# Masked convolution and test-time-training scan: the mask's moments as two fused passes, its parts on ScalarE, statistics of two images first

## The reference

```
sumX = max(x.sum((2, 3)), 1e-9)
mu_x = max(round((ix * x).sum((2, 3)) / sumX), 1)      # ix = 1..28 down, iy across
mu_y = max(round((iy * x).sum((2, 3)) / sumX), 1)
m = |posX - mu_xg| + |posY - mu_yg|
m = max(1 - m * mask_weight, -1)
out = conv3x3(max(x * m, 0)) + bias
```

## Time and profile before

| what | value |
|---|---|
| median of 3 runs | 1995.46 us (1990.15 to 1995.93) |
| profiled execution | 1991.81 us, its span 1989.7 us |
| PE busy in the span | 1620.6 us (81%) |
| DVE | 1579.8 us (79%) |
| POOL | 1315.9 us (66%) |
| ACT | 991.3 us (50%) |
| granted TensorE clock, mean | 0.643 |

### The profile page before, as it was taken

How to read it: one execution, slowest core, us unless ns; L and a number is a source line. 1 busy time by engine, 2 the same in 40 slices (tenths; PEclk the granted TensorE clock), 3 DMA queues, 4 the chain that set the end, 5 groups by cost and what they waited for, 6 DMA issues and landing times.

```text
span 1989.7 us, 82066 instructions
## 1 busy us (share of the span) xinstructions
PE 1620.6 (81%) x33520; PEld 1206.9 (61%) x33520; DVE 1579.8 (79%) x3721; ACT 991.3 (50%) x2358; POOL 1315.9 (66%) x1479
## 2 busy tenths in 40 slices
PE   1886978922798889888888888888888898888886
PEld 1443544511676667767667667667676676676674
DVE  6999997704788788888888887887888887888864
ACT  2223545443455555555555555555555555555553
POOL 1244535365687787777777777777777777777763
PEclk9997999965555655555555556655566555655555
DMA  6058696963465665675665665665656656666554
GB/s 238 1 30 45 97 97 68 81 148 69 52 76 68 71 80 69 74 78 67 73 79 68 73 73 70 76 72 68 80 65 73 79 68 72 73 70 76 67 61 49
DMA packets 1650518, 148.80 MB, mean 75 GB/s; under 512 B 1630176, under 2 KB 1643744, under 8 KB 1650144
## 3 DMA queue, kind: packets, MB, share of 16 engines
q1 hardware_dynamic: 1390640, 117.87, 51.0%
q10 hardware_dynamic: 259504, 25.70, 10.7%
HBM read 40.71 MB, written 38.54 MB: 40 GB/s over the span
## 4 chain that ended last, share of the span: by engine, by line
SPq 24%; PE 16%; DVE 15%; DMA 10%; issue 7%; ACT 3%; DVEq 0%; POOL 0%; ACTq 0%; POOLq 0%
SPq L477 16%; DMA kqk<-work 8%; SPq L493 7%; PE p_kt L1624 6%; PE p_x L1668 4%; DVE work L1303 2%; DMA late<-work 2%; DVE work L1270 2%; DVE work L1294 2%; PE p_m L1653 2%; DVE work L1363 1%; PE p_x L1659 1%; DVE work L1385 1%; DVE zs L1350 1%; DVE m L1357 1%
## 5 line engine op out<-in xcount | busy, mean ns | idle before, releaser
L795 ACT ACTIVATE work<-p_kt 128x512 f16<-128x512 f32 x196 | 149.1, 761 | 213.7 <-PE p_kt L1624 212.9
L1624 PEld LDWEIGHTS p_kt<-fold,kqk 128*128 128x128 f16 x6272 | 185.0, 104 | 97.2 <-ACT work L795 46.1
L1624 PE MATMUL p_kt<-fold,kqk 128*128 128x16 f16 x6272 | 200.6, 175 | 52.8 <-DMA kqk<-work 45.0
L1597 PE MATMUL p_j<-wa,work 128*128 128x512 f16 x196 | 119.5, 610 | 146.9 <-DVE work L1270 102.2
L621 POOL TENSOR_TENSOR work<-work,rope_s 128x256 f32<-128x256 f32 x196 | 161.5, 844 | 83.8 <-DVE work L1270 83.8
L592 POOL TENSOR_TENSOR work<-work,g 128x256 f32<-128x256 f32 x98 | 71.8, 732 | 201.7 <-DVE work L1341 198.8
L1303 DVE TENSOR_TENSOR work<-work 128x256 f16<-128x256 f32 x196 | 164.3, 893 | 15.8 <-ACT work L782 15.8
L1532 PE MATMUL p_j<-work 128*128 128x392 f16 x864 | 157.7, 344 | 23.3 <-DVE work L1117 20.7
L1668 PEld LDWEIGHTS p_y<-w,late 128*128 128x128 f16 x4704 | 145.7, 103 | 17.9 <-issue 8.5
L1668 PEld LDWEIGHTS p_x<-w,late 128*128 128x128 f16 x4704 | 149.0, 105 | 12.3
L1597 PEld LDWEIGHTS p_j<-wa,work 128*128 128x128 f16 x196 | 24.9, 127 | 207.4 <-issue 176.6
(11 more groups left out here) (173 smaller groups left out, 4397.4 us busy)
## 6 DMA issues: line engine op xcount, KB each, us to landing
kqk<-work SPq DMA_DIRECT2D x392, 64.0 KB, 4.7
late<-work SPq DMA_DIRECT2D x392, 64.0 KB, 3.8
late<-work SPq DMA_DIRECT2D x392, 32.0 KB, 2.6
out_y<-work ACTq DMA_DIRECT2D x49, 256.0 KB, 6.8
x_scratch<-late SPq DMA_DIRECT2D x24, 392.0 KB, 11.8
xs_scratch<-work SPq DMA_DIRECT2D x24, 392.0 KB, 6.5
work<-x_scratch ACTq DMA_DIRECT2D x49, 192.0 KB, 3.6
work<-xs_scratch SPq DMA_DIRECT2D x48, 192.0 KB, 2.8
```

Of the source, the lines that this page charges most:

```text
L795: return act.activation(kqt16[:, o, g:g + GP, :, :, :].rearrange("p g h t a -> p g a (h t)"), p_kt[:, :].rearrange("p (g a n) -> p g a n", ...
L1597: pe.matmul(p_j[k][:, 0:4 * C], tokens(s, k, 0), wa16[:, :], start=True, stop=False, skip_group_check=True)
L1624: mm = pe.matmul(p_kt[:, at:at + CS], part_of(g + k, h, a), fold16[:, :], start=True, stop=True)
```

## The change

Image sums: `normalise` lets ACT add up the image it writes (`accum_out=tot`). The two reductions, the weighting and the two moment reductions become two passes over 784 elements on DVE, each with an accumulated sum. The rounding subtraction disappears into a ramp that already holds the rounding constant. Absolute value and the two mask parts move from DVE to ACT, as `mask_parts(n)`. On ACT `scaled(k)` now stands before `relu(b + 2)` instead of behind it. The first statistics batch is images 0 and 1, the second images 2 to 7; numbers of later batches rise by one. The core of the diff:

```
 normalise(b):
-    act.activation(gx, image, Identity, bias=gshift, scale=gscale)
+    act.activation(gx, image, Identity, bias=gshift, scale=gscale, accum_out=tot[:, b % 4:b % 4 + 1])
+def mask_parts(b):                               # on ACT
+    act.wait_ge(cv_v.sem, cv_v.count("dist", b))
+    act.activation(flat, flat, ACT.Abs).then_inc(cv_m.sem, 1)
+    act.wait_ge(cv_m.sem, cv_m.count("absd", b))
+    act.activation(ab[:, p, 0, :], ab[:, p, 0, :], ACT.Identity, bias=eps_s[:, 4:5], scale=mwn[:, 0:1])...
+    act.activation(ab[:, p, 1, :], ab[:, p, 1, :], ACT.Copy, scale=mwn[:, 0:1])...
 ACT, round b:
     normalise(b + 3); add_bias(b + 3)
     if i == 4 and q < NG - 1: gn_root(...)
     if i == 1 and q > 0: gn_root(...)
+    mask_parts(b + 2)
+    for k in scaled_at(b): scaled(k)
     relu(b + 2)
-    for k in scaled_at(b): scaled(k)
 DVE:
-    dve.tensor_reduce(rc[:, 0, :], img2, AX.X, ALU.add)
-    dve.tensor_reduce(rc[:, 1, :], img2.rearrange("c i j -> c j i"), AX.X, ALU.add)
-    dve.tensor_tensor(rcw, rc, ramp_s, ALU.mult)
-    dve.tensor_reduce(cen[:, 0:2], rcw, AX.X, ALU.add)
-    dve.tensor_reduce(cen[:, 2:3], rc[:, 0, :], AX.X, ALU.add)
+    dve.scalar_tensor_tensor(out=prod, in0=img2, scalar=1.0, in1=<row ramp, broadcast>, op0=mult, op1=mult, accum_out=cen[:, 0:1])
+    dve.scalar_tensor_tensor(out=prod, in0=img2, scalar=1.0, in1=<column ramp, broadcast>, op0=mult, op1=mult, accum_out=cen[:, 1:2])
-    mask_round, mask_absd, mask_parts             # L1029, L1044, L1051, L1052
 POOL mask_sum(b):
-    pool.wait_ge(cv_v.sem, cv_v.count("col_part", b))
+    pool.wait_ge(cv_m.sem, cv_m.count("col_part", b))
 DVE before the loop:
-    statistics of 0..7; gn_centre, gn_scale of 0..7; mask and masked of 0, 1; weight split
+    stats_first(0), (1); gn_centre, gn_scale of 0..1; mask_point(0); stats_first(2); weight split; masked(0);
+    mask_point(1); stats_first(3), (4); masked(1); stats_first(5), (6), (7); gn_centre, gn_scale of 2..7
 PE, b = 0:
+    conv_half(0, 0); wait statistics of 7; gn_mean(1); conv_half(0, 1); gn_var(1)
 ACT before the loop:
+    normalise(0), (1); weights; mask_parts(0); add_bias(0); mask_parts(1); relu(0); add_bias(1); relu(1); gn_root(1); normalise(2)
```

More of the change, by code:

```diff
@@ L269, in program @@
         cv_s = steps("conv_scalar", "relu high")
-        cv_v = steps("conv_mask_vector", "rows cols weigh moment total floor inv ratio magic round dist absd row_part col_part masked")
+        cv_v = steps("conv_mask_vector", "rows cols floor inv ratio magic dist masked")
+        cv_m = steps("conv_mask_scalar", "absd row_part col_part")
         cv_p = steps("conv_pool", "mask lo")
@@ L723, in scaled @@
                 act.activation(xs16[:, b % 2, :, 0], xs32[:, b % 2, :], ACT.Copy).then_inc(xs_a.sem, 1)
-            gn_root(0, 0, GB)
+            gn_root(0, 0, 2)
             act.wait_ge(gn_v.sem, gn_v.count("shift", 0))
             normalise(0)
+            normalise(1)
+            act.wait_ge(s_convw, 16)
+            act.activation(convw16[:, 0, :, :], convw_s, ACT.Copy, scale=CONV_SCALE).then_inc(cw.sem, 1)
+            mask_parts(0)
             add_bias(0)
-            normalise(1)
+            mask_parts(1)
+            relu(0)
             add_bias(1)
+            relu(1)
+            gn_root(1, 2, GB - 2)
+            act.wait_ge(gn_v.sem, gn_v.count("shift", 1))
             normalise(2)
             add_bias(2)
[L733 to L736, removed]
             for b in range(B):
@@ L1100, in _, with mask_point @@
                 stats_kept(b)
-            gn_centre(0, 0, GB)
-            gn_scale(0, 0, GB)
-            for b in range(2):
-                mask_sums(b)
-                mask_weigh(b)
-                mask_moment(b)
+            def mask_point(b):
+                mask_rows(b)
+                mask_cols(b)
                 mask_floor(b)
@@ L1110, in _ @@
                 mask_magic(b)
-                mask_round(b)
                 mask_dist(b)
-                mask_absd(b)
-                mask_parts(b)
-                masked(b)
+            stats_first(0)
+            stats_first(1)
+            gn_centre(0, 0, 2)
+            gn_scale(0, 0, 2)
+            mask_point(0)
+            stats_first(2)
             dve.wait_ge(cw.sem, cw.count("high", 0))
@@ L1118, in _ @@
                                      in1=convw16[:, 0, :, :], op0=ALU.mult, op1=ALU.subtract).then_inc(cw.sem, 1)
+            masked(0)
+            mask_point(1)
+            stats_first(3)
+            stats_first(4)
+            masked(1)
+            stats_first(5)
+            stats_first(6)
+            stats_first(7)
+            gn_centre(1, 2, GB - 2)
+            gn_scale(1, 2, GB - 2)
             done = [0]
@@ L1242, in _ @@
             dve.wait_ge(ev_v.sem, ev_v.count("aggr", B - 1))
[L1243 to L1244 removed]
+            gn_centre(8, GB * (NG - 1), GB)
+            gn_scale(8, GB * (NG - 1), GB)
             def zero_late():
```

141 lines of the change are left out of this document (65 added, 76 removed).

## The result

The changed kernel takes 2001.42 us (median of 20 runs, 1993.83 to 2016.97) against 1992.82 us of the kernel before in the same comparison (20 runs, 1986.31 to 1998.86). The ratio is 1.0048, 95% interval 1.0032 to 1.0064: 9.6 us slower by the ratio (6.4 to 12.8), 8.6 by the two medians. The prediction was 2008 us and slower. The profiled execution has a span of 2000.0 us against 1989.7.

A forecast was written before the change was run, and what follows sets the result against it. In the stage up to 410 us, neither PE nor DVE bounded throughout; a loop through ACT, POOL and stores set later images. Terms 6 - 7 - 4.3 - 7.5 - 3 = -15.8, 16 us slower: 2008 us, range 1983 to 2025.

The forecast's parts named there:

- masked 2: Head: first product near 30 us, but image 2's masking 1 us later than now; bounds 4 later to 3 earlier.
- The gain up to image 15: Before the scaled-before-relu losses: shorter rounds of images 2 to 9 and +1 for images 10 to 15, gain 6 us.
- Pairs: Rounds scaling two images: relu waits behind ACT's copy for a store; 7 us lost from 15 to 18, 7.5 from 23 to 26.
- Group stores: Store 8 lands late behind group 1's eight stores, ACT's copy of image 10 waits and holds relu 22; 4.3 us lost.
- everything is as before: Images 10 to 15, after POOL's memset: nothing changes but the short gn_var wait of 2 us; +1 us in all.
- The tail: Image 18 behind group 2's stores holds relu 30; the last scaled_low and POOL's memset come 3 us later.
- Passes, read-out: New DVE moment passes: between 0.9 and 1.6 us each, taken as 1.0; accumulator read-out at most 0.19 us.
- half-rate rival: Rival: DVE's accumulating pass runs at half an element per cycle, 0.9 us more a pass; 2034 us, chance 0.10.
- Passes beside POOL: New passes with two SBUF inputs and GpSimd lock each other out; if so, relu_low begins up to 0.5 us later each round.
- A loop through ACT, POOL and the stores: Said to set the 11 us per image in images 15 to 18, 18 to 23 and 23 to 26, not PE.
- The stores are in time: Rival: a pair's second store lands in 6.5 us or the relu is not due, so pairs cost nothing; 1982 us, chance 0.18.
- A wash: Rival: pairs cost half and the head gives 3 us, -4 in sum or its mirror; 1996 us, chance 0.16.

The follow-up runs named there:

- e1: The changed kernel with scaled(k) put back behind relu(b + 2) on ACT; 1985.3 us, ratio 0.9965 to the kernel before.
- e2: The kernel before with only scaled(k) put in front of relu(b + 2); 2014.2 us, ratio 1.0111 to the kernel before.
- e4: The changed kernel, order as changed, with three buffers of xs16 instead of two; 1968.7 us, ratio 0.9885 to the kernel before.
- e3: The kernel before with moments as two passes, total from ACT and parts on ACT, order and head as before; 1981.2 us, ratio 0.9945.
- e11: The kernel before with moments as two passes and total from ACT, absolute value and parts still on DVE; 1974.9 us, ratio 0.9914.
- e12: Old head, two-pass moments, three buffers, residual stores spread, scaled behind relu, absolute value and parts on DVE; 1963.3 us, ratio 0.9864 to the kernel before.
- e6: The kernel before with three buffers of xs16 and nothing else; 1979.4 us, ratio 0.9932 to the kernel before.
- e5: The changed kernel with three buffers of xs16 and scaled(k) behind relu(b + 2) again; 1965.8 us, ratio 0.9866 to the kernel before.

## Why the prediction was right, and where it was off

**The mechanism.** It was right in place and kind. e1, e2 and e4 show it from three sides: take the order away and 16 us come back, put it alone into the kernel before and 22 us go, take away most of what makes ACT wait and the same order costs some 3 us by the medians, not told from nothing.

**The terms**, at the places where they were forecast (plus is a gain, minus a loss, in us):

| term | predicted | measured |
|---|---|---|
| masked 2 | 1 later | 0.7 earlier |
| images 2 to 9 | +6 | +5.3 |
| images 9 to 15 | +1 | +3.5 |
| 15 to 18 | -7 | -6.5 |
| 18 to 23 | -4.3 | -4.2 |
| 23 to 26 | -7.5 | -6.6 |
| 26 to the stage's end | -3 | -5.6 |
| sum at the stage's end | -15.8 | -13.3 |

- *Pairs.* The chain was counted almost to the tenth: relu 16 late by 3.3 us (3 predicted), relu 17 by 7.8 (7.6), masked 18 ends 39.6 us behind masked 15 (40.1).
- *Group stores.* 4.2 us in the trace. But e1 shows that only 2.2 of them belong to the order; 2.0 are paid with the order undone as well: 1.1 because the store lands later behind masked 18 (0.8 was forecast), 0.9 because mask_parts stands behind the same wait. The prediction asked what is queued behind L734 and named the relu; it did not name the next round's parts.
- *The gain up to image 15* is the term that was mis-sized, 6 predicted against 9.6. Of the 3.6 us that were missing, 1.7 stand at masked 2 and 2.5 between images 9 and 15; between 2 and 9 the gain was 0.7 smaller than forecast. The moments alone give 11.6 us (e3), the new head takes some of it back. The head was priced as one shorter chain to masked 2; that it leaves PE idle for 11 us and that the products then run at 0.50 of the clock was not in the sum, although the forecast of an early image 1 and a late image 2 implied the pause. The 2.5 us behind image 9 are a single round behind the memset: from masked 11 to masked 12 it takes 8.8 us against 11.6, where "everything is as before" was expected. By e11 and e12 some 2 us of it belong to the parts on ACT.
- *The tail.* 5.6 against 3. ACT waits 14.69 us in front of relu 30, then 7.00 us in front of image 21's copy (5.50 and 5.06 at the same two places before): the last group's stores queue up behind one another. With the order undone the stretch takes 79.1 us (e1), as before (79.7).
- *The sum.* That it came within 2.5 us is in part luck: a gain forecast 3.6 us too small and a tail forecast 2.6 us too small stand against each other.
- *Passes, read-out.* 0.97 us and 0.08 us, 1.05 together against the 1.0 taken. The half-rate rival is out. The Trainium skill (Vector Engine (DVE) Microarchitecture Reference, § 7. Points that are easy to get wrong) has such an instruction at half its throughput; here the pass with an accumulated sum takes 975 ns and the same form without one 974 (L1057), and L992, which reads only one tensor of 784 elements, takes 0.97 us too. So the measurement decides against it for this case; one input of the pass is a ramp of 28 elements read again and again, that of L1057 a full tensor.
- *Passes beside POOL.* relu_low was forecast to begin up to 0.5 us later in a round. It begins in time, but its row is longer: L539 takes 1.84 us on average, L537 took 1.64; what makes it longer no run takes apart. The rows that the prediction called on for this lock do not show that form of it: L1019 there reads one tensor and a scalar, and POOL's memset reads none.
- *The bound of the pace.* "A loop through ACT, POOL and the stores" was wrong for rounds with two scaled images in the old order: e6 removes the store wait and the 33 us stay. By the rows of e5 and e6, DVE's small instructions beside POOL set them; no run tests that apart.

**From the stage to the whole.** The stage ends 13.3 us late, but 9.6 us are measured. From the stage's end to the span's end the 14 profiled executions of this study take 1563.4 to 1573.8 us, in no order with what stands ahead. One execution can so give or take several us in the scan, which no edit touches. In the two profiled executions it is 3.0 us (1571.4 before, 1568.4 changed), and their spans differ by 10.3. Whether the whole difference between 13.3 and 9.6 is that, or the stage's own loss differs from run to run too, stays open: there is one trace of each kernel.

**The rivals.** "The stores are in time" falls at once: the pair landed 9.3 us after its scaled_low, ACT waited 48.8 us. "A wash" had the gain about right (9) and the losses half; they came in full.

## What to carry to other kernels

On an in-order queue an instruction that can wait for a store must stand behind the one that PE's next work hangs on, and when that cannot be, the buffer count decides: one more buffer took the price of the order from some 20 us to some 3 by the medians, not told from nothing. When a bulk store of a group shares the issuing queue with the small stores that free buffers, spread it: in the changed kernel, with two buffers, that alone was worth 20 us, with three buffers 7 us at the stage's end and nothing that the times can tell. And a shorter chain on DVE pays only up to the point where another queue's order decides, so read first what is queued behind each wait on every engine that the edit loads, the newly moved instructions included.

## What was not expected of the hardware

- DVE's read-out of an accumulated sum takes 0.08 us, ACT's 0.19 us, and the accumulating pass itself no longer than a plain one (975 and 974 ns).
- Not only instructions with two SBUF tensors are held by POOL. L1040 reads two elements of one tile and lasts 1.85 us beside scaled_low (the rows under e6), 0.14 us when POOL is idle, as in this row of e1; the statistics next to it keep their 0.55 us. The Trainium skill (SBUF — State Buffer, § SBUF: two separate sides) names a second class for the same lock, DVE instructions in a mode with two ports; L1040's rows would fit it; which mode it ran in no row shows.

```profile
80.48 0.14 DVE L1040 TENSOR_SCALAR work<-work 128x2 f32<-128x2 f32 x1
```

- A pause of PE costs beyond its length: after 7.9 us without a product the granted clock was 0.50, the lower level, for the next 4.4 us (first row the pause, then what follows), and image 17's first half took 7.4 us instead of 4.75.

```profile
232.94:240.86 7.92, 0.01 (x1) 0.00 (x0) 3.63 (x15) 5.00 (x7) 1.67 (x2) 0.70 0.60 130
240.86:245.29 4.43, 4.43 (x14) 2.07 (x15) 0.00 (x0) 1.01 (x4) 4.43 (x3) 0.50 0.35 38
```
